# Causal mask of an attention stage: from a product on VectorE after the exp to two matmuls on TensorE before it

## The reference, cut to what matters

```python
scores = jnp.einsum('bhqd,bhkd->bhqk', q, k) / math.sqrt(HD)
mask = jnp.tril(jnp.ones((Sq, Sq), dtype=bool))
scores = jnp.where(mask, scores, jnp.finfo(scores.dtype).min)
attn = jax.nn.softmax(scores, axis=-1)
y = jnp.einsum('bhqk,bhkd->bhqd', attn, v)
```

## Time and profile before

| what | value |
|---|---|
| two timed runs, median | 6779.56 us (6638.66 and 6920.45) |
| profiled execution | 6495.98 us |
| its span, slowest core (core 0) | 6494.3 us |
| spans of the 8 cores | 6456.1 to 6494.3 us |
| mean granted TensorE clock, 8 cores | 0.829 to 0.832 |
| TensorE matmul busy | 4663.8 us (72%), 18,896 instructions, and as many weight loads |
| VectorE busy | 1634.4 us (25%) |
| ScalarE busy | 1815.9 us (28%) |
| loop of `attn_b` | from 3011 to 4909 us of the span, prologues of the pairs among it |

### The profile page before, as it was taken

One profiled execution on the slowest core, in us unless ns is written; L12 is line 12 of the kernel. 1 busy time (PEld: TensorE's weight loads), 2 busy tenths in 40 slices (PEclk: granted clock), 3 DMA queues, 4 the chain that ended last, 5 costly groups with the idle time before them and its releaser, 6 DMA issues.

```text
span 6494.3 us, 57075 instructions; the slowest of 8 cores (6456.1 to 6494.3 us)
## 1 busy us (share of the span) xinstructions
PE 4663.8 (72%) x18896; PEld 1701.5 (26%) x18896; DVE 1634.4 (25%) x2990; ACT 1815.9 (28%) x2414; POOL 81.8 (1%) x158
## 2 busy tenths in 40 slices
PE   2599677758997777575676676676775555997787
PEld 0133222213443333231111111121111112443333
DVE  4444445540001222224213213213212440000000
ACT  1101000103330000003675675665672002330000
POOL 0000000000001000000000000000000000001000
PEclk6799788878998888796886877876877777998998
DMA  3200211123226333200000000000003224226333
GB/s 91 39 1 1 65 39 39 52 56 93 75 75 143 104 102 102 54 0 4 4 6 6 4 6 5 4 6 5 5 6 89 82 91 103 75 76 156 110 104 117
DMA packets 259276, 356.30 MB, mean 55 GB/s; under 512 B 20341, under 2 KB 168053, under 8 KB 256694
## 3 DMA queue, kind: packets, MB, share of 16 engines
q1 hardware_dynamic: 237462, 304.53, 14.5%
q0 software_dynamic: 21536, 48.12, 4.5%
HBM read 257.96 MB, written 142.74 MB: 62 GB/s over the span
## 4 chain that ended last, share of the span: by engine, by line
PE 57%; DVE 13%; ACT 12%; DMA 7%; issue 5%; DVEq 2%; ACTq 1%; POOL 1%; SPq 0%; another core or an unknown queue 0%; POOLq 0%
PE f2pyo L580 7%; ACT expb L853 7%; PE f1pyo L580 6%; PE f1pph L533 6%; PE f2pph L533 6%; PE py L822 4%; PE psc L841 3%; PE py L826 2%; PE pr L950 2%; DVE xnt L235 2%; PE ppt L485 2%; PE ppk L313 2%; PE ppb L467 2%; PE p L679 2%; PE ppv L321 2%
## 5 line engine op out<-in xcount | busy, mean ns | idle before, releaser
L853 ACT ACTIVATE expb<-psc 128x1024 bf16<-128x1024 f32 x896 | 889.9, 1024 | 235.1 <-PE psc L845 226.5
L822 PE MATMUL py<-expb,vpair 128*65 128x512 bf16 (+3 forms) x1152 | 475.5, 413 | 393.3 <-ACT expb L853 271.2
L580 PE MATMUL f2pyo<-f2hb,f2w 128*128 128x512 bf16 x2048 | 462.5, 390 | 133.2 <-DMA f2hb<-scr_h 114.1
L580 PE MATMUL f1pyo<-f1hb,f1w 128*128 128x512 bf16 x2048 | 474.0, 396 | 52.3 <-DVE xnt L235 23.9
L533 PE MATMUL f1pph<-xnt,f1w 128*128 128x512 bf16 x2048 | 448.9, 381 | 65.9 <-DMA f1w<-w 61.6
L533 PE MATMUL f2pph<-xnt,f2w 128*128 128x512 bf16 x2048 | 448.8, 380 | 62.1 <-DMA f2w<-w 56.0
L841 PE MATMUL psc<-xnt,kpair 64*128 64x512 bf16 (+3 forms) x1152 | 479.1, 417 | 8.2 <-DVE vpair L776 8.2
L845 PE MATMUL psc<-xnt,kpair 64*128 64x512 bf16 (+3 forms) x1152 | 479.3, 418 | 0.0
L826 PE MATMUL py<-expb,vpair 128*65 128x512 bf16 (+3 forms) x1152 | 476.6, 414 | 0.0
L864 DVE TENSOR_TENSOR expb<-expb,trim 128x128 bf16<-128x128 bf16 x256 | 57.7, 225 | 1320.5 <-ACT expb L858 1317.9
L856 ACT ACTIVATE expb<-psc 128x512 bf16<-128x512 f32 (+3 forms) x256 | 112.3, 439 | 776.9 <-PE psc L845 774.9
(11 more groups left out here) (196 smaller groups left out, 4666.1 us busy)
## 6 DMA issues: line engine op xcount, KB each, us to landing
p_xf<-xT SPq DMA_DIRECT2D x16, 2048.0 KB, 9.7
scr_h<-f1hs SPq DMA_DIRECT2D x256, 128.0 KB
f1hb<-scr_h SPq DMA_DIRECT2D x64, 512.0 KB, 9.3
scr_h<-f2hs SPq DMA_DIRECT2D x256, 128.0 KB
f2hb<-scr_h SPq DMA_DIRECT2D x64, 512.0 KB, 9.0
scr<-p_x1f SPq DMA_DIRECT2D x8, 2048.0 KB, 6.9
f1xf<-scr SPq DMA_DIRECT2D x8, 2048.0 KB, 14.4
scr<-f1x2f SPq DMA_DIRECT2D x8, 2048.0 KB, 8.0
```

What stands on the lines that cost most here:

```text
L580: ins = T.matmul(pyo[ot][:, :], w2s[jt][:, ot * 128:ot * 128 + 128], hb[gi][:, jj * 512:jj * 512 + 512], start=(jt == 0), stop=(jt == NJ - 1))
L822: T.matmul(py0[0:65, pcol0:512], vpair[:, pt * 130:pt * 130 + 65], expb[pbank][:, pcol0:512], start=(pt == 0), stop=(pt == plast))
L853: exp_free[bank] = ss.inc(Sc.activation(expb[bank][:, :], psc[bank][:, :], AF.Exp, scale=0.125))
```

## The change

In a diagonal tile the mask is put on the scores before the exp, by TensorE, and the two products on VectorE go.

Behind each head's scores comes a product of `lmat` (as weights) and `ident` that adds -1e9 to the masked places in the same PSUM columns: `start=False` adds to what stands there, and the scores' own product no longer carries `stop=True`. The exp makes 0 of them. The waits for `mask_done` fall away on TensorE, before the scores and before y, since `exp_mask` is always None. `trim` is still loaded. Full tiles stay as they were.

```diff
                         self.w(T, ss, exp_free[bank])
-                        if m >= 0:
-                            self.w(T, sv, mask_done[bank])
                         T.matmul(psc[bank][:, col0:512],
                                  kpair[0:64, tsl],
                                  self.xnt[p][0:64, c * 512 + col0:(c + 1) * 512],
-                                 start=True, stop=True)
+                                 start=True, stop=(m < 0))
+                        if m >= 0:
+                            T.matmul(psc[bank][:, col0:col0 + 128], self.lmat[:, :],
+                                     self.ident[:, :], start=False, stop=True)
                         ins = T.matmul(psc[bank][:, 512 + col0:1024],
                                        kpair[64:128, tsl],
                                        self.xnt[p][64:128, c * 512 + col0:(c + 1) * 512],
-                                       start=True, stop=True)
+                                       start=True, stop=(m < 0))
+                        if m >= 0:
+                            ins = T.matmul(psc[bank][:, 512 + col0:512 + col0 + 128],
+                                           self.lmat[:, :], self.ident[:, :],
+                                           start=False, stop=True)
                         e_sc = st.inc(ins)
...
-                        if m >= 0:
-                            self.w(V, ss, exp_free[bank])
-                            V.drain()
-                            V.tensor_tensor(expb[bank][:, col0:col0 + 128],
-                                            expb[bank][:, col0:col0 + 128],
-                                            trim[:, :], ALU.mult)
-                            mask_done[bank] = sv.inc(V.tensor_tensor(
-                                expb[bank][:, 512 + col0:512 + col0 + 128],
-                                expb[bank][:, 512 + col0:512 + col0 + 128],
-                                trim[:, :], ALU.mult))
-                            exp_mask = mask_done[bank]
-                        else:
-                            exp_mask = None
+                        exp_mask = None
```

## The result

The changed kernel is slightly slower: the ratio of its time to the kernel before is 1.0044, with a 95% interval of 1.0028 to 1.006. The ratio makes some +29 us; the medians of all executions are 6533.89 us (43) and 6503.78 us (42). In both kernels, and in the experiments, some executions are 2 to 6% longer with one die or both granted less clock; the ratios leave them out, the two timed runs of before on whose median of 6779.56 the prediction stood were of this kind, and where a profile is touched I read the other die's cores. The profiled executions are 6528.3 and 6495.98 us, +32. The changed kernel's slowest core is core 6, with a span of 6526.6 us; the eight span 6483.4 to 6526.6, mean clock 0.835 to 0.837.

The account below looks back on a forecast made before the run. It took a latency chain of scores, exp and y through TensorE and ScalarE to bound the loop. Terms +8 + 22 - 22 = +8 us on the 6779.56 median gave 6788 us; range 6440 to 6930, effect alone -75 to +80.

Parts of the forecast that it names:

- What bounds the loop: Third-stage attention loop: a ring of latencies through TensorE and ScalarE with two buffers, 1.12 us a full tile at 2.4 GHz.
- The chain of 4.87 us: Diagonal group of four tiles at 2.4 GHz: scores, exp, mask and y in sequence through tiles 0 and 2 fill 4.87 us.
- Price of a transition, 0.10 us: On TensorE, each change between products of 64 and 128 rows in a diagonal tile costs 0.10 us, bounds 0 and 0.28.
- Rival 1: Row changes around the mask products cost more than 0.10 us; at 0.28, +137 us, or 6917; chance 0.13.
- Rival 3: Mask products don't interrupt the scores, halves stay side by side in diagonal tiles: some -60 us, 6720; chance 0.07.
- A group at 2.4 GHz, +0.13: Diagonal group at full clock: +1.13 us of scores against -1.00 of mask wait, about 5.00 us; 52 groups.
- 12 groups at 1.2 GHz at +1.85, +22: Diagonal groups at low clock: TensorE alone is full, 7.76 us instead of 5.83; 12 such groups, +22 us.
- my first two terms: Cost in the diagonal groups: +8 us for 52 at 2.4 GHz and +22 us for 12 at 1.2 GHz.
- What the clock gives back, -22: Around diagonals: denser TensorE streaming removes 12 of 56 low-clock stretches, 1.8 us each, -22 us; bounds 0 and -101.
- Rival 2: Denser diagonals keep the clock up at all 56 places: -71 us, 6709 (-1.0%); chance 0.15.
- Rival 4: The mask holds the diagonal chain less, 0.70 us a group instead of 1.00: +27 us, 6807; chance 0.10.
- The footing and the sum: Whole kernel: +8 us in sum, 6504 on the profiled execution, given as 6788 on the median of two timed runs.

## Why the prediction was wrong

- **What bounds the loop**: right. The chain of 4.87 us, its 0.50 for the mask and its two tiles of four were measured as they were worked out (no mask: 3.86 against 3.87).
- **Price of a transition, 0.10 us**: right, 0.10 to 0.11 at 2.4 GHz beside products of 128 columns too. Rival 1 (0.28) fell. Rival 3 (no interruption) is what the 64-row products do, not the 128-row ones.
- **A group at 2.4 GHz, +0.13**: right for the group read, 5.02 us; on average over the five later groups of a pair it was +0.07. At 1.2 GHz I had 7.76; 7.57 and 6.9 to 7.3 came.
- **12 groups at 1.2 GHz at +1.85, +22**: nearly right in sum and by chance. 16 are at 1.2 GHz, since the second group of each pair, which before got its clock back in time in part of the pairs, no longer does. The first ones cost 1.10 each and not 1.85, the second ones 1.98, 24.6 us together. With those at 2.4 GHz that is +27.3 where my first two terms said +30.
- **What the clock gives back, -22**: the step that failed. I let 12 of 56 slow stretches vanish. None did. They got shorter, 513 us of slow time in the loops to 454 (in the diagonal groups it grew from 88 to 118, among the full tiles it fell from 422 to 336), but the time saved was the cheap part. A stretch began 0.6 us after the tail's first instruction on average before and 3.2 us after it now (320 places each, single ones from 3 us before it to 5 behind it). So before it lay more over the 2.2 us in which TensorE waits for ScalarE's denominators anyway, and now it lies more over full tiles, at 1.54 instead of 1.12 us each. The traces show it: over the first three tiles of chunks 1 to 7, the wait among them, slow time fell by 94 us a core (241.6 to 147.9) and the time by only 5.6 (341.6 to 336.0); over the other full tiles slow time rose by 8 (180.2 to 188.3) and the time by 3.0 (862.3 to 865.3). That gave 2.5 us back instead of 22. My price of 1.8 us a stretch took all 6.8 us as full tiles; more than half of the slow time among the full tiles (241.6 of 421.8 us) lay in the first three, where it costs little. The later start comes with the wait for the mask gone, and not with the streaming that I had argued from: the run without a mask has it at 3.0 us, the one with both masks at 0.5. Why the clock falls later then, no run shows.
- **Rival 2** (all 56 back) has the wrong condition: denser diagonals turned no fall away, the gap had to be filled, which I named as the argument against it. Filled, it is worth 93 us of loop where I had 101 for all; 72 of them are in the full tiles, 20 in the second groups of the pairs.
- **Rival 4** fell with the run without a mask.
- **The footing and the sum**: I put the time on the median of two runs that stood 4% too high, so 6788 is no measure of the kernel; on the profiled execution I had 6504, and 6528 came. The loops grew by 27.2 us where I had 8: 19.5 of the difference lie in the clock's term, 2.4 in the last groups of the pairs, which I hadn't priced, and 2.7 go the other way in the groups' terms. The chance of 0.88 for within 2% is borne out; the effect, +29 us and clear of no change, is over three times the +8 that I forecast.

## What to carry to other kernels

Before a step moves from a waiting engine to TensorE, write down what stands next to it in TensorE's queue: two 64-row products that run side by side are parted by one full product between them, and the order of four products was worth 74 us here, more than the whole of the change. A stretch of low clock is worth what lies in it, not its length; look which engine waits there. Where TensorE has a regular gap behind another engine's work, unused products in it can pay; a run with the same products elsewhere tells whether the place matters.

## What the runs showed that I had not expected

- Products of 64 rows on different halves run side by side even with other 64-row products written between them (3117.76, 3117.77, 3117.99, 3118.00): the engine doesn't hold them to the written order's neighbours.
- Adding 1024 weight loads and matmuls to the kernel before made its slow time grow, from 513 to 578 us. The diagonal groups hold 46 of the 65, mostly the first two of a pair, which are at 1.2 GHz and longer there (7.76 and 7.69 us instead of 6.05 and 5.59); 17 lie among the full tiles, and where these come from I didn't try.
- A 128-column score product right behind another one takes 0.07 us at 2.4 GHz with its weight load, so splitting a product in two cost 0.02 us on the chain.
